# Attention and token-mix kernel on one core: first chunk reordered, 24 tiles a batch turned by DMAs, input normalised on GpSimd

## The reference

```python
# x: (8, 1024, 256)
xn = layernorm(x)
x = x + attention(xn) + ffn(xn)

def attention(x):                     # 8 heads, one shared key/value head of 128
    q = (x @ Wq + bq) + pe            # per head 128 wide
    k, v = split(x @ Wkv + bkv); k = k + pe
    probs = softmax(causal(q @ k.T / sqrt(128)))
    return (probs @ v) @ Wo           # heads side by side

def ffn(x):
    x_prev = shift(x)                 # the token before, zero for the first
    xr = mu_r * x + (1 - mu_r) * x_prev
    xk = mu_k * x + (1 - mu_k) * x_prev
    return sigmoid(xr @ W_r.T) * (square(relu(xk @ W_k.T)) @ W_v.T)
```

## Time and profile before

| | before |
|---|---|
| time, median of 3 runs | 1562.81 us (1562.58 to 1563.08) |
| the profiled execution | 1561.37 us |
| its span in the profile | 1559.6 us |
| PE, PEld busy | 1533.5 us, 1497.6 us |
| DVE, ACT, POOL busy | 1210.4 us, 1056.2 us, 1060.7 us |

### The profile page before, as it was taken

One profiled execution on the slowest core, in us unless ns is written; L12 is line 12 of the kernel. 1 busy time (PEld: TensorE's weight loads), 2 busy tenths in 40 slices (PEclk: granted clock), 3 DMA queues, 4 the chain that ended last, 5 costly groups with the idle time before them and its releaser, 6 DMA issues.

```text
span 1559.6 us, 35317 instructions
## 1 busy us (share of the span) xinstructions
PE 1533.5 (98%) x12032; PEld 1497.6 (96%) x12032; DVE 1210.4 (78%) x3284; ACT 1056.2 (68%) x2531; POOL 1060.7 (68%) x1549
## 2 busy tenths in 40 slices
PE   5999999999999999999999999999999999999998
PEld 5999999999999999999999999999999999999998
DVE  6888767887678876788768787688876888768875
ACT  5776667766667766677577676676766677666764
POOL 5666776667756777567775676756766577765765
PEclk8999999999999999999999999999999999999999
DMA  4014420244202441024410244103431034300443
GB/s 139 9 53 121 146 75 22 58 122 148 69 15 69 129 143 55 15 75 134 144 42 15 86 141 127 42 15 98 140 129 32 12 112 138 129 20 8 119 147 105
DMA packets 151425, 132.46 MB, mean 85 GB/s; under 512 B 12240, under 2 KB 146512, under 8 KB 151248
## 3 DMA queue, kind: packets, MB, share of 16 engines
q1 hardware_dynamic: 150672, 129.55, 27.0%
q10 hardware_dynamic: 576, 0.66, 0.1%
HBM read 67.25 MB, written 62.91 MB: 83 GB/s over the span
## 4 chain that ended last, share of the span: by engine, by line
PE 76%; POOL 10%; issue 7%; DVE 5%; ACT 1%; DMA 0%; POOLq 0%; DVEq 0%; ACTq 0%
PE pS L893 25%; PE pO L893 23%; PE pG L893 19%; PE pT L986 8%; POOL qt L450 3%; POOL X L506 3%; DVE gate L698 1%; POOL pt L465 1%; POOL mh L456 1%; DVE X L872 1%; POOL rstd L434 1%; DVE mix L742 1%; POOL v L444 1%; POOL X L505 1%; DVE pt L797 1%
## 5 line engine op out<-in xcount | busy, mean ns | idle before, releaser
L893 PE MATMUL pO<-pt,v 128*128 128x256 f32 x3456 | 466.6, 285 | 6.5 <-DVE ot L848 5.3
L893 PE MATMUL pS<-kt,qt 128*128 128x288 f32 (+41 forms) x2304 | 458.6, 329 | 2.0 <-POOL qt L450 2.0
L659 ACT ACTIVATE X<-X,bias 128x16 f32<-128x16 f32 (+56 forms) x512 | 375.9, 734 | 93.3 <-DVE bias L872 92.8
L893 PEld LDWEIGHTS pO<-pt,v 128*128 128x128 f32 x3456 | 426.1, 189 | 12.1 <-DVE ot L848 10.0
L872 DVE CUSTOM_DVE_ANT_0 X<-pS,mask 128x16 f32<-128x16 f32 (+56 forms) x512 | 353.8, 691 | 45.1 <-issue 22.9
L506 POOL TENSOR_SCALAR X<-X,rec 128x16 f32<-128x16 f32 (+56 forms) x512 | 367.0, 717 | 23.0 <-DVE rec L780 23.0
L893 PEld LDWEIGHTS pS<-kt,qt 128*128 128x128 f32 x2304 | 367.5, 190 | 14.0 <-issue 2.2
L465 POOL TENSOR_TENSOR pt<-Z,pt 128x640 fp32r<-128x640 f32 (+3 forms) x128 | 256.6, 2005 | 63.3 <-ACT pt L588 61.6
L797 DVE TENSOR_TENSOR pt<-pT,pt 128x512 fp32r<-128x512 f32 (+3 forms) x512 | 257.3, 522 | 26.6 <-ACT pt L595 23.7
L595 ACT CAST pt<-pT 128x512 fp32r<-128x512 f32 (+3 forms) x512 | 223.0, 461 | 61.7 <-PE pT L986 58.8
L652 ACT CAST ot<-pO 128x256 fp32r<-128x256 f32 x256 | 96.2, 376 | 241.2 <-PE pO L893 115.0
(11 more groups left out here) (101 smaller groups left out, 1788.6 us busy)
## 6 DMA issues: line engine op xcount, KB each, us to landing
park_dram<-Y SPq DMA_DIRECT2D x32, 512.0 KB, 2.6
Z<-park_dram SPq DMA_DIRECT2D x128, 128.0 KB, 2.8
park_dram<-Y SPq DMA_DIRECT2D x32, 448.0 KB, 3.0
Z<-park_dram SPq DMA_DIRECT2D x128, 112.0 KB, 2.5
park_dram<-Y SPq DMA_DIRECT2D x32, 384.0 KB, 2.9
Z<-park_dram SPq DMA_DIRECT2D x128, 96.0 KB, 2.3
park_dram<-Y SPq DMA_DIRECT2D x32, 320.0 KB, 2.7
Z<-park_dram SPq DMA_DIRECT2D x128, 80.0 KB, 2.1
```

Of the source, the lines that this page charges most:

```text
L659: nc.scalar.activation(x_row(s, 0, w), x_row(s, 0, w), ACT.Exp, bias=bias[:, j:j + 1], scale=-1.0, accum_out=total[:, j:j + 1]).then_inc(e ...
L893: last = nc.tensor.matmul(out, a[i], m[j], start=start and k == 0, stop=stop and k == n - 1)
```

## The change

- `turned(s)` holds from step 16 on: 24 steps a batch instead of 16. The buffers grow: `Y` has two, `park_dram` four slots, and the read-back of a tile is issued one turn after its write-out (`fetch`, `park` in place of `move`). Which row of `X` a step uses is a table of 64 entries (`HALVES`), and before a row is written DVE waits for the very transpose that read it (`turned_before`).
- `norm_apply` moves from DVE to POOL (two 128x256 instructions a chunk).
- `xnt` and `xt` have one buffer instead of two; ACT waits for their readers.
- Within a turn PE makes the WO product first, then the other fillers, then the product with `v`. DVE takes the fillers' results before statistics and mix instead of after.
- `LEAD` is 10 instead of 12; entries of `TURNS`, `WO_AT` and `AT` move by 1 to 5 turns.
- The first chunk: `wkv`, the biases and small parts of the position tables are loaded from ACT's queue, `wq` comes first on SP's; `wr`, `wv` go to free parts of `X`, `wo` to `Y`, and are split in turns 2, 6 and 8 to 11 instead of 1 to 6. The low part of `xt` is made by DVE from PSUM, that of `wq1` by POOL, the low parts of q are shared by DVE (first head of a pair) and POOL (second). `START` uses five banks. PE starts with 20 transposes of `ident` into `pO` (`WARM`), whose result is not used.
- `scaled_by_act` is never true, so what depends on it is not in the program.

The diff, cut to its core:

```diff
-H_LAG = 7
-L_LAG = 7
+H_LAG = (7, 6)
+L_LAG = (7, 7)
+C_LAG = 2
 QTMP = 2
-LEAD = 12
+LEAD = 10
 PER = TPC * H
 LAST_IT = STEPS + LEAD
+WARM = 20
 SHARED = NT // 2 * H
...
+      "mixr_dve": (0, 1, 1, 0),
       "mixr_out": (3, 2, 4, 1),
...
-START = [("XT", 0, 0), ("KV", 0, 0), ("KT", 0, 0)] + [("Q", 0, p) for p in range(PAIRS)]
...
+    return HALVES[s], 1 if s < SHARED else 2
...
 def turned(s):
 
-    return s >= SHARED and s % 2 == 0
+    return s >= 16 and s % 2 == 0
...
+def turned_before(s):
+
+    j, n = halves_of(s)
+    found = []
+    for half in range(j, j + n):
+        back = 1
+        while not halves_of((s - back) % STEPS)[0] <= half < sum(halves_of((s - back) % STEPS)):
+            back += 1
+        if turned((s - back) % STEPS):
+            found.append((TURNED.index((s - back) % STEPS), s < back))
+    return found
...
+G_BANK = dict(zip(START, (0, 1, 2, 3, 4, 0, 2)))
 for k, u in enumerate([u for it in range(SHARED) for u in FILL[it]]):
     G_BANK[u] = (k + 1) % 3
+
...
-            load("wkv", wkv_d)
             load("wq0", wq_d[:, 0:H * D // 2])
-            sp.dma_start(kpos[:, :, :], petok_d.rearrange("(n p) d -> p n d", p=P)).then_inc(k_terms_loaded, 16)
+            load("wq1", wq_d[:, H * D // 2:H * D])
             load("wk", wk_d)
-            load("wq1", wq_d[:, H * D // 2:H * D])
+            sp.wait_ge(w_loaded["wq1"], 16)
+            sp.dma_start(xtok[:, 1, :, :], x_v[1, :, :, :]).then_inc(x_loaded[1], 16)
+            sp.dma_start(kpos[:, TPC:NT, :], petok_v[:, TPC:NT, :]).then_inc(k_terms_loaded[1], 16)
             load("wr", wr_d)
+            sp.dma_start(pet[:, CHUNK:T], pet_d[:, CHUNK:T]).then_inc(q_terms_loaded[1], 16)
             load("wv", wv_d)
...
-            def move(b, s):
-
-                k = turned_no(b, s)
-                slot, nk = k % 2, s // H + 1
+            def park(b, s):
+
+                k, nk = turned_no(b, s), s // H + 1
                 sp.wait_ge(turned_ready, k + 1)
-                if k >= 2:
-                    sp.wait_ge(landed[slot], 64 * (k // 2))
-                sp.dma_start(park_d[slot, :, :, 0:nk * 32],
-                             Y[:, :, 0:nk, :].rearrange("p a k c -> p a (k c)")).then_inc(parked, 16)
+                if k >= 4:
+                    sp.wait_ge(landed[k % 4], 64 * (k // 4))
+                sp.dma_start(park_d[k % 4, :, :, 0:nk * 32],
+                             Y[:, k % 2, :, 0:nk, :].rearrange("p a k c -> p a (k c)")).then_inc(parked[k % 2], 16)
+
+            def fetch(b, s):
+
+                k, nk = turned_no(b, s), s // H + 1
+                sp.wait_ge(parked[k % 2], 16 * (k // 2 + 1))
                 if k >= 2:
                     sp.wait_ge(turned_lo, k - 1)
-                sp.wait_ge(parked, 16 * (k + 1))
                 for q in range(4):
-                    sp.dma_start(Z[32 * q:32 * (q + 1), slot, :, 0:nk, :].rearrange("r a k c -> r a (k c)"),
-                                 park_d[slot, :, q, 0:nk * 32].rearrange("(a r) n -> r a n", a=4)
-                                 ).then_inc(landed[slot], 16)
+                    sp.dma_start(Z[32 * q:32 * (q + 1), k % 2, :, 0:nk, :].rearrange("r a k c -> r a (k c)"),
+                                 park_d[k % 4, :, q, 0:nk * 32].rearrange("(a r) n -> r a n", a=4)
+                                 ).then_inc(landed[k % 4], 16)
 
             for b, it in turns():
+                if it - V_LAG - 1 in TURNED:
+                    fetch(b, it - V_LAG - 1)
+                if it - V_LAG in TURNED:
+                    park(b, it - V_LAG)
                 for r in [r for r in range(NT) if min(WO_AT[r] + 1, LAST_IT - 1) == it]:
                     store(b, r // TPC, r % TPC)
                 for r in [r for r in range(1, NT, TPC) if min(WO_AT[r] + 4, LAST_IT - 1) == it]:
                     if b < B - 1:
                         reload(b, r // TPC)
-                if it - V_LAG in TURNED:
-                    move(b, it - V_LAG)
             for c in range(NC):
                 sp.wait_ge(stored[c], 16 * TPC * B)
 
...
+            def norm_apply(n, slot):
+                pool.wait_ge(rstd_ready, n + 1)
+                for t in range(TPC):
+                    nc.gpsimd.tensor_scalar(xn[:, t, :], xtok[:, slot, t, :], mv[:, t, 0:1], rstd[:, t:t + 1],
+                                            ALU.subtract, ALU.mult).then_inc(xn_ready, 1)
+
...
-            split_xt(0, 0)
-            pool.wait_ge(k_terms_loaded, 32)
-            nc.gpsimd.tensor_tensor(kpos[:, :, :], kpos[:, :, :],
-                                    bkv[:, 0:D].rearrange("p (a n) -> p a n", a=1).broadcast_to((P, NT, D)),
-                                    ALU.add).then_inc(kpos_ready, 1)
+            norm_apply(0, 0)
+            key_terms(0, 0, TPC)
+            pool.wait_ge(w_hi["wq1"], 1)
+            nc.gpsimd.tensor_tensor(W["wq1"][1], STAGE["wq1"], W["wq1"][0].bitcast(F), ALU.subtract
+                                    ).then_inc(w_lo["wq1"], 1)
             split_v(0, 0)
+            split_q(0, 0, 0, 1, 2)
             split_mix(0, 0)
-            for p in range(PAIRS):
-                split_q(0, 0, p, 0)
-                split_q(0, 0, p, 1)
+            for p in range(1, PAIRS):
+                split_q(0, 0, p, 1, 2)
             for b, it in turns():
                 turn(b, it)
+                if b == 0 and it == 1:
+                    key_terms(1, TPC, NT)
...
+            act.dma_start(STAGE["wkv"], wkv_d.rearrange("(t p) n -> p t n", p=P)).then_inc(w_loaded["wkv"], 16)
+            act.dma_start(bkv[:, :], bkv_d).then_inc(k_terms_loaded[0], 16)
+            act.dma_start(kpos[:, 0:TPC, :], petok_v[:, 0:TPC, :]).then_inc(k_terms_loaded[0], 16)
             act.dma_start(mu[:, :], mu_d).then_inc(mu_loaded, 16)
-            act.dma_start(bkv[:, :], bkv_d).then_inc(k_terms_loaded, 16)
-            act.dma_start(bq[:, :], bq_d).then_inc(q_terms_loaded, 16)
-            act.dma_start(pet[:, :], pet_d).then_inc(q_terms_loaded, 16)
+            act.dma_start(bq[:, :], bq_d).then_inc(q_terms_loaded[0], 16)
+            act.dma_start(pet[:, 0:CHUNK], pet_d[:, 0:CHUNK]).then_inc(q_terms_loaded[0], 16)
...
             weight_hi("wkv", slice(0, CT))
+            weight_hi("wq0", slice(0, CT))
             xt_out(None, 0)
+            weight_hi("wk", slice(0, CT))
             act.wait_ge(xnt_ready, 1)
             act.wait_ge(xnt_zero, 1)
             act.wait_ge(omu_ready, 1)
-            mix_before(0, 0, 0)
-            weight_hi("wq0", slice(0, CT))
-            weight_hi("wq1", slice(0, CT))
+            mix_before(0, 0)
+            v_out(None, 0)
             kt_out(None, 0)
-            v_out(None, 0)
+            q_out(None, 0, 0)
             mix_out(0, 0)
-            weight_hi("wk", slice(0, CT))
-            for p in range(PAIRS):
+            for p in range(1, PAIRS):
                 q_out(None, 0, p)
...
-            nc.vector.memset(xnt[:, 0, :, 0:1], 0.0).then_inc(xnt_zero, 1)
-            norm_apply(0, 0)
+            nc.vector.memset(xnt[:, :, 0:1], 0.0).then_inc(xnt_zero, 1)
+            dve.wait_ge(mu_loaded, 16)
+            nc.vector.tensor_scalar(omu[:, :], mu[:, :], -1.0, 1.0, ALU.mult, ALU.add).then_inc(omu_ready, 1)
+            dve.wait_ge(tri_made, 4)
+            nc.vector.tensor_reduce(mask[:, T - SUB:T], steps_of[:, :, :].rearrange("p h c -> p c h"),
+                                    mybir.AxisListType.X, ALU.max).then_inc(tri_ready, 1)
...
+            def split_first(p):
+                dve.wait_ge(q_hi, p + 1)
+                nc.vector.tensor_tensor(qt[1][:, 0, :, 2 * p, :],
+                                        qtmp[:, p % QTMP, 0, :].rearrange("p (t q) -> p t q", q=SUB),
+                                        qt[0][:, 0, :, 2 * p, :].bitcast(F), ALU.subtract).then_inc(q_first, 1)
+
             weight_lo("wkv", slice(0, CT))
-            dve.wait_ge(mu_loaded, 16)
-            nc.vector.tensor_scalar(omu[:, :], mu[:, :], -1.0, 1.0, ALU.mult, ALU.add).then_inc(omu_ready, 1)
+            dve.wait_ge(xt_first, 1)
+            nc.vector.tensor_tensor(xt[1][:, :, :], g_bank("XT", 0, 0).rearrange("p (t n) -> p t n", t=CT),
+                                    xt[0][:, :, :].bitcast(F), ALU.subtract).then_inc(xt_ready, 1)
             weight_lo("wq0", slice(0, CT))
-            weight_lo("wq1", slice(0, CT))
-            dve.wait_ge(kpos_ready, 1)
+            dve.wait_ge(kpos_ready[0], 1)
             kv_out(None, 0)
-            token_mix(0, 0, 0)
+            weight_lo("wk", slice(0, CT))
             kt_out(None, 0)
-            dve.wait_ge(q_terms_loaded, 32)
+            dve.wait_ge(q_terms_loaded[0], 32)
             q_out(None, 0, 0)
-            weight_lo("wk", slice(0, CT))
+            token_mix(0, 0)
+            split_first(0)
             q_out(None, 0, 1)
             q_out(None, 0, 2)
+            split_first(1)
             q_out(None, 0, 3)
-            dve.wait_ge(tri_made, 4)
-            dve.wait_ge(consts, 4)
```

(23 more changed lines are left out.)

318 lines of the change are left out of this document (179 added, 139 removed).

## The result

| | before | the change |
|---|---|---|
| time, median | 1562.81 us (1562.34 to 1563.24, 5 runs) | 1569.98 us (1567.29 to 1572.33, 5 runs) |
| the profiled execution, its span | 1561.37, 1559.6 us | 1570.45, 1568.7 us |
| first scores of batch 0, of batch 1, of batch 7 | 27.14, 204.28, 1352.09 | 25.51, 208.19, 1359.18 |

The account below looks back on a forecast made before the run. PE's own work was taken as the bound after the beginning. The terms -27.1 + 3 - 1 - 5.5 = -30.6 us gave 1530.8 us profiled, 1532.2 us as median, 2.0% faster; range 1519 to 1547.

Parts of the forecast that it names:

- What bounds the kernel: From about turn 9 of the first batch PE's own work; before the first scores, latency of a chain over all engines.
- Transposes, -27.1 us: 224 of PE's 1472 transposes go, at 121 ns each: 27.1 us saved, bounds 18.6 and 34.3.
- What the turned tiles cost the others: DVE, ACT, POOL: POOL rises to 1164 us, DVE falls to about 1160; hidden by PE's products, counted as nothing.
- the new chain, +3 us: Short turns 16 to 31: turned tiles arriving late add 0.4 us of PE waits a batch, +3 us, bounds 0 and 16.
- The worst tile is that of step 16: Its transpose, write-out, read-back, cast and low part take 8.0 us, leaving 1.2 us of slack before the product with v.
- The norm on POOL, 0.48 us an instruction: Layernorm moved from DVE costs POOL about 64 x 0.48 = 31 us, priced by a scaling of nearly that width.
- WO ahead of the product with v, -1 us: Fills PE's wait for DVE's ot; of 5.3 us perhaps 1 goes, bounds 0 to -5.
- The first chunk, -5.5 us: First scores 5.0 us earlier, near 22 us, plus 0.5 us from moved weight splits; bounds -1 and -9.
- splits ... no longer sit in turns 1 to 6: Splits of wr, wv, wo on ACT and DVE leave the turns after turn 0: 0.5 us gained.
- The 20 buy nothing: Transposes in front do not count as PE activity, so KV stays at the low clock; otherwise 1.4 us more gained.
- Rival 4: Slower: each of 8 tiles a batch holds PE up 0.6 us beyond its saving, 1567 us; chance 0.05.
- the sign of error named: PE waits for masks or turned_lo over 0.5 us in turns 18 to 31, or PE's remaining products taking longer.

Follow-up runs that it names:

- run 5: The change with POOL's power (inv_std) and norm both moved behind the scaling of the turn; 1543.4 us, ratio 0.9884 to the kernel before.
- run 7: run 5 with 16 turned tiles a batch in place of 24 and the earlier table of rows; 1559.3 us, ratio 0.9984 to the kernel before.
- run 12: run 5 with POOL's norm as four instructions with one pointer scalar each in place of two with two; 1562.0 us, ratio 1.0002 to the kernel before.
- run 13: run 11 with POOL's norm as multiply by 1/std, then subtract a shift (mean times 1/std); 1542.9 us, ratio 0.9881 to the kernel before.
- run 14: run 11 with POOL's norm as two multiplications, so the norm is not computed; 1534.2 us, ratio 0.9823 to the kernel before.
- run 16: run 15 with POOL's norm as multiply by 1/std, then add a shift, with two small instructions more; 1532.1 us, ratio 0.9804 to the kernel before.
- run 15: run 11 with the splits of wo in turns 3, 4, 5 and 7 of batch 0 instead of 8 to 11; 1539.4 us, ratio 0.9859 to the kernel before.
- run 9: run 5 with chunk 0's norm on DVE, mu first on ACT's queue, POOL's split of wq held until xt is there; 1541.9 us, ratio 0.9871.
- run 10: run 9 without the 20 transposes in front (WARM = 0); 1542.0 us, ratio 0.9872 to the kernel before.
- run 11: run 9 with the norm of the first batch's second chunk on DVE too; 1540.9 us, ratio 0.9869 to the kernel before.
- run 1: The change with the norm on DVE again, behind its statistics; 1560.0 us, ratio 0.9994 to the kernel before.
- run 4: The kernel before with 24 turned tiles a batch and their table of rows, old order, norm on DVE, one Y buffer; 1593.2 us, ratio 1.0204.

## Why the prediction was wrong

**What bounds the kernel** was read rightly, and so was its condition, "as long as the others keep up". They did not.

**Transposes, -27.1 us.** The sign and the mechanism hold, the size was too large: 19 to 21 us (86 to 93 ns each, runs 5 and 7), close to the lower bound, the 83 ns read from PE's timeline. The weight loads fell by the 27.0 us forecast and the busy time by 33.9, but neither is what PE gives up. The Trainium skill (Trainium Kernel Development and Optimization, Performance Expectations) prefers the LDWEIGHTS share to matmul busy time; it was the nearer of the two here and still a third too large.

**What the turned tiles cost the others, and the new chain, +3 us: the steps that failed.** "No engine becomes the bound over a batch, so these costs count as nothing" took shares of a batch for an answer about a place. "The worst tile is that of step 16" followed one tile through the read-back. There ACT stands for `Z` as forecast, 1.3 to 1.9 us in seven of the eight batches and 2.9 in one, but PE shows no wait of over 0.5 us for a mask or a low part in those turns (its longest, 0.54 us, is for the norm). The tile that hurt was that of step 30: it meets the statistics, the power and the norm of the next chunk, and the WO addition behind DVE's transpose. That the engines cross (POOL waits for DVE's statistics, DVE for POOL's scaling) was not asked, though the earlier trace rows had DVE at 7.85 of 8.05 us just before, and the earlier trace rows had its 29.0 us of waits for the power. PE's idle time went from 0.7 to 3.6 us a batch, 2.9 us more in place of 0.4: 23 us in eight batches, and the lower clock behind the gaps cost 4 to 5.

**The norm on POOL, 0.48 us an instruction.** It takes 1.22 us in turn 32 of the change and 1.29 in the mean. The row it was taken from the earlier trace rows has nearly the width, but another operation, and runs 12, 13, 14 and 16 show that the operation decides. That is no detail: with 0.58 us for the same result the kernel gains 7.3 us (run 16 against 15).

**WO ahead of the product with v, -1 us.** PE's wait for DVE's `ot` ahead of the product with `v` fell from 5.3 us to 1.3; instead PE waits for ACT's `ka` before it can use bank `pG` (3.5 us). No net gain is visible, and no run separated it.

**The first chunk, -5.5 us.** First scores came 1.6 us earlier, not 5.0, and two later places took back more than that. The norm on POOL costs 2.43 us ahead of `XT` where DVE took 0.9 (run 9), and DVE stood until 8.9 us for `mu`, with its split of `wkv` behind it. The third scores wait 3.43 us for the second chunk's norm (before, 2.2 us lay between the second and third scores, now 4.7). And "splits ... no longer sit in turns 1 to 6" was counted as a gain of 0.5 us; those of `wo` went to turns 8 to 11, where DVE is full; from the scores of step 10 to those of step 16 it takes 2.2 us longer than before (run 15 took 1.7 of them back).

**The transposes in front.** "The 20 buy nothing" was nearly right for the change, whose KV takes 2.90 us, and wrong as a rule. In run 9 they bring KV to 1.62 us, where run 10 without them has 2.90. The rule behind it, that a transpose does not count as PE-busy the same way as a product (the Trainium skill, TensorE: Matmul & The Clock Gate, Part 4), is contradicted by that pair of runs. In the change too the four transposes of `XT` behind the 20 took 0.67 us, where they took 1.08 before, but the granted clock fell again at 10.6 us, ahead of KV. The value of the 20 for the whole time was not measurable all the same.

**The sum.** -20 for the transposes, +23 waits, +4.5 clock, and for the beginning -1.6 + 2.4 + 2.2 = +3.0: +10.5 us, against 9.1 measured between the spans; 1.4 us are not placed. Rival 4 came nearest in its number (1567), by another mechanism: not eight tiles at 0.6 us each, but one gap of 2 us in each batch. Of what the profile was to show, POOL came to 1212.8 us in place of 1164 (the norm) and DVE to 1167.0 in place of 1160; the count of 1248, the 27 us of weight loads and KV at 240 ns a matmul (2.90 us for 12) were there; a batch 3.3 us shorter was not, and PE was busy 98.0% of the time after 41 us, not within 1% of always; the sign of error named, waits "in turns 18 to 31", looked just short of the place. That run 16 ends at the predicted 1532 us is not a confirmation: it is luck, since it mends things that the prediction had not seen, and its terms are other ones.

## What to carry to other kernels

When a change puts an instruction at a fixed place in one in-order queue, and it waits for another queue, list what stands ahead of its releaser there, and what waits for the first queue in turn: a loop of two queues costs where no share shows it. An operation that nobody waits for goes behind the one that somebody waits for; here that order alone was worth 26.6 us between the medians (the change against run 5). An order that costs nothing with one set of tiles can cost much with another: with 16 tiles the same move gave 3.3 us. And price an instruction by a row with the same operation, not only the same width.

## What was not expected of the hardware

- GpSimd's `tensor_scalar` on 128x256 fp32: 0.58 to 0.59 us as multiply and multiply or multiply and add, 1.18 to 1.31 us as soon as a subtraction is one of the two (runs 11 to 14 and 16).
- DVE's norm instruction (two tensor inputs in SBUF, 128x256) took 0.47 to 0.65 us in the 33 cases of run 1 in which POOL was not at an instruction with two tensor inputs, and 0.86 to 2.07 us in the 31 in which it was. It is not so for every pair: DVE's split of a transposed tile, which has one input in PSUM, took 0.64 to 0.69 us either way.
- The granted clock fell to half 0.4 to 1.3 us after gaps of 1.9 us in otherwise full work, in three of eight such gaps (the change), and behind six of eight gaps of 2.8 us (run 4); behind the eight of 1.6 us in run 1 it never fell. And the granted clock does not tell all: in run 10 KV took its 2.90 us in a stretch with a granted clock of 1.00.

```profile
8.00:12.00 4.00, 2.51 (x12) 2.24 (x11) 2.07 (x3) 3.34 (x6) 2.72 (x2) 1.00 0.89 262
```
